# Last block of a recommendation kernel: its final scale on ScalarE and its store from ScalarE's queue, in place of VectorE and SP's queue

## The reference

```python
x_reg = input_data @ W_lin.T + b_lin
emb = input_data @ factors                      # 12500 -> 16
sum_squared = jnp.square(emb.sum(axis=1))
squared_sum = (jnp.square(input_data) @ jnp.square(factors)).sum(axis=1)
h = jax.nn.relu(emb @ W1.T + b1)                # 16 -> 128
h = jax.nn.relu(h @ W2.T + b2)                  # 128 -> 64
dnn_out = h @ W3.T + b3                         # 64 -> 1
x = x_reg + 0.5 * (sum_squared - squared_sum)[:, None] + dnn_out
x = 0.5 + jax.nn.sigmoid(x) * 5.0
return x.squeeze()
```

## Time and profile before

| what | value |
|---|---|
| three runs | 133.61, 133.75, 133.87 us |
| profiled execution, its own time | 133.76 us |
| its span, first to last instruction | 132.0 us |
| PE busy | 107.0 us (81%) |
| ACT busy | 61.5 us (47%) |
| DVE busy | 52.6 us (40%) |
| moved by DMA | 52.36 MB, mean 397 GB/s |
| mean granted TensorE clock | 0.974 |

### The profile page before, as it was taken

How to read it: one execution, slowest core, us unless ns; L and a number is a source line. 1 busy time by engine, 2 the same in 40 slices (tenths; PEclk the granted TensorE clock), 3 DMA queues, 4 the chain that set the end, 5 groups by cost and what they waited for, 6 DMA issues and landing times.

```text
span 132.0 us, 2607 instructions
## 1 busy us (share of the span) xinstructions
PE 107.0 (81%) x1123; PEld 34.6 (26%) x1123; DVE 52.6 (40%) x51; ACT 61.5 (47%) x52; POOL 15.7 (12%) x48
## 2 busy tenths in 40 slices
PE   6099969429979839749749979999998987989992
PEld 4012222002212112112112233322222112345881
DVE  0391063027036036046045016565351351576571
ACT  4030067029039039049048046868562561465851
POOL 3015000200010200200200110164530000000000
PEclk9999999995999999999977999999999999999999
DMA  3999899989999998998999999899999999999700
GB/s 106 413 531 417 377 477 472 407 387 467 427 387 462 457 427 387 457 437 387 467 457 427 387 457 447 377 432 412 452 407 407 462 415 417 418 404 411 302 26 1
DMA packets 3489, 52.36 MB, mean 397 GB/s; under 512 B 404, under 2 KB 536, under 8 KB 1560
## 3 DMA queue, kind: packets, MB, share of 16 engines
q1 hardware_dynamic: 3480, 52.23, 93.2%
HBM read 52.22 MB, written 0.00 MB: 396 GB/s over the span
## 4 chain that ended last, share of the span: by engine, by line
DMA 54%; PE 40%; SPq 2%; DVE 1%; issue 1%; ACT 1%
DMA xr<-in_x_pairs 43%; PE p_lin L506 34%; DMA xr<-in_x_end 11%; PE p_sq L506 2%; PE p_h L601 2%; SPq L273 1%; PE p_tot L506 1%; PE p_h L632 1%; PE p_tot L614 0%; DVE h L454 0%; DVE h L449 0%; SPq L267 0%; SPq L266 0%; PE p_tot L621 0%; SPq L265 0%
## 5 line engine op out<-in xcount | busy, mean ns | idle before, releaser
L327 ACT ACTIVATE sq<-xr 128x2560 f32<-128x2560 f32 x20 | 45.9, 2333 | 46.8 <-DMA xr<-in_x_pairs 38.8
L427 DVE TENSOR_TENSOR sq<-xr 128x1536 f32<-128x1536 f32 x20 | 34.6, 1761 | 53.7 <-DMA xr<-in_x_pairs 42.9
L506 PE MATMUL p_lin<-xr,wr 128*17 128x512 f32 x320 | 39.9, 638 | 15.6 <-DMA xr<-in_x_pairs 14.4
L506 PE MATMUL p_lin<-sq,wz 128*18 128x512 f32 x320 | 37.7, 592 | 0.0
L506 PEld LDWEIGHTS p_lin<-xr,wr 128*17 128x17 f32 x320 | 9.2, 102 | 44.5 <-issue 38.4
L307 POOL COPY wr<-hd 128x136 f32 (+1 forms) x20 | 9.3, 464 | 75.0 <-PE p_lin L506 75.0
L506 PEld LDWEIGHTS p_lin<-sq,wz 128*18 128x18 f32 x320 | 10.1, 98 | 25.8 <-issue 25.0
L506 PE MATMUL p_lin<-xr,hd 128*17 128x352 f32 (+1 forms) x128 | 10.0, 380 | 1.3 <-DMA xr<-in_x_end 1.3
L437 DVE TENSOR_TENSOR sq<-xr 128x1408 f32<-128x1408 f32 (+3 forms) x6 | 6.6, 1135 | 6.1 <-DMA xr<-in_x_end 6.1
L337 ACT ACTIVATE sq<-xr 128x1408 f32<-128x1408 f32 (+3 forms) x6 | 5.7, 983 | 6.3 <-DMA xr<-in_x_end 6.3
L506 PE MATMUL p_lin<-sq,ws 128*18 128x352 f32 x64 | 6.6, 459 | 0.0
(11 more groups left out here) (52 smaller groups left out, 40.8 us busy)
## 6 DMA issues: line engine op xcount, KB each, us to landing
xr<-in_x_pairs SPq DMA_DIRECT2D x8, 4096.0 KB, 21.9
xr<-in_x_groups SPq DMA_DIRECT2D x4, 2048.0 KB, 18.3
xr<-in_x_end SPq DMA_DIRECT2D x1, 2112.0 KB, 10.5
xr<-in_x_end SPq DMA_DIRECT2D x3, 640.0 KB, 12.0
xr<-in_x_end SPq DMA_DIRECT2D x1, 1760.0 KB, 14.3
xr<-in_x_end SPq DMA_DIRECT2D x1, 1056.0 KB, 12.4
hd<-in_head SPq DMA_DIRECT2D x1, 952.0 KB, 4.8
xr<-in_x_end SPq DMA_DIRECT2D x1, 704.0 KB, 13.7
```

The source lines that it names most:

```text
L327: nc.scalar.activation(sq[:, ring(s), BY_DVE:CHUNKS, :], xr[:, s, BY_DVE:CHUNKS, :], ACT.Square).then_inc(act_squared, 1)
L427: nc.vector.tensor_tensor(sq[:, ring(s), 0:BY_DVE, :], xr[:, s, 0:BY_DVE, :], xr[:, s, 0:BY_DVE, :], ALU.mult).then_inc(dve_squared, 1)
L506: return nc.tensor.matmul(out, lhsT, rhs, start=False, stop=False, skip_group_check=True)
```

## The change

For blocks 0 and 1 nothing is changed. For block 2, the last, VectorE's scale is taken out. ScalarE waits for its own sigmoid, computes Copy(5.0 * sg + 0.5) into `y`, waits for that, and issues the store itself, from its own DMA queue. SP's loop of stores is one shorter; its last wait still counts the landings of all three.

```diff
@@ sync
-            for k in range(len(BLOCKS)):
+            for k in range(LAST):
                 sp.wait_ge(y_ready[k], 1)
                 sp.dma_start(out[cols(k)].rearrange("(q b) -> q b", q=4), y[0:P:32, line(k)]).then_inc(y_stored, 16)
             sp.wait_ge(y_stored, 16 * len(BLOCKS))
@@ scalar
             nc.scalar.copy(qs[:, :], p_sq[:, 0:BLOCKS[LAST][1]]).then_inc(qs_ready, 1)
             sigmoid(2)
+            act.wait_ge(sg_ready[2], 1)
+            nc.scalar.activation(y[:, line(2)], sg[:, line(2)], ACT.Copy, bias=0.5, scale=5.0).then_inc(y_ready[2], 1)
+            act.wait_ge(y_ready[2], 1)
+            nc.scalar.dma_start(out[cols(2)].rearrange("(q b) -> q b", q=4), y[0:P:32, line(2)]).then_inc(y_stored, 16)
@@ vector
             layer1(2, p_h1[1], BLOCKS[2][1])
             layer2(2)
-            scale(2)
```

## The result

The changed kernel took 133.99 us (median of 20 runs, 133.85 to 134.23) against 133.75 us before (20 runs, 133.61 to 134.01). The ratio is 1.0017, with a 95% interval of 1.001 to 1.0024: slower by 0.24 us, within the 0.2% that I called no change, and clear of zero. The forecast was 133.91.

The account below looks back on a forecast made before the run. Input DMA (54%) and TensorE (40%) bound the kernel; only its serial 2.5 us tail could change. Scale +0.03, hand-overs 0, issue +0.13, landing 0 gave +0.16 us: 133.91, 8 in 10 from 133.55 to 134.40.

Parts of the forecast that it names:

- The place: Tail of 2.5 us behind TensorE's last adds at 129.47: all steps in series, each nanosecond counting in the kernel's time.
- The scale: Block 2's scale on ScalarE instead of VectorE: 215 ns for 185, +0.03 us, ends +0.02 and +0.11.
- The wait of an engine for itself: ScalarE's semaphore wait between its sigmoid and scale: 0.03 us as across engines, so 0; ends 0.03 less, 0.05 more.
- The hand-over to the DMA: From the scale's end to the store's issue: 0.04 us, taken the same on ScalarE, so 0.
- The queue: Last store on ScalarE's own queue: no gain, 0, since SP had nothing before it but its wait.
- The issue: ScalarE's issue of the last store, priced like SP's first store: 0.63 for 0.50, +0.13 us, ends -0.17 and +0.68.
- landing: From the last store's issue to its landing: taken as 0, low end -0.25 us (0.86 in place of 1.11).
- rival A: ScalarE's first DMA is dear: up to +0.71 us, named 134.18, deciding from an issue of 0.74 us; chance 0.41.
- The sum: All terms of the tail together: +0.16 us, 133.91 us, +0.12%, within the 0.27 us called the same.
- The closing barrier: Kernel's end: ScalarE's drain at about 130.6 instead of 129.5, 1.0 us before SP passes its wait, so not moved.

Follow-up runs that it names:

- one step more: Changed kernel plus one more ACTIVATE on ScalarE, copying y onto itself with a wait, between scale and store: 134.26 us, ratio 1.0031 to the kernel before.
- the two halves: Against the kernel before: ScalarE scales block 2, SP stores it, 133.88 us (1.0003); VectorE scales, ScalarE stores it, 133.92 us (1.0007).
- the second group: Changed kernel unaltered, run again beside the kernel before on the same chip: 133.99 us against 133.84, ratio 1.0006.

## Why the prediction was right, and where not

*The place.* Only the tail moved, and it is serial: confirmed, with one step more of 265 ns by forecast and 263 to 268 got out in the branch (2533 against 2270 and 2265).

*The scale, forecast +0.03.* It was 236 - 185 = 51 ns. My straight line through squares of 160 and 320 columns gave 215, and the Trainium skill's estimate (page "ScalarE: Activation LUTs", section "What ACT_TABLE_LOAD costs") 219; the measurement is above both, inside the range of 0.02 to 0.11.

*The wait of an engine for itself, forecast 0.* The scale starts 326 ns after the sigmoid's start on either engine: exactly 0. The hand-over to the DMA is 29 ns in both, and 25 and 32 in the two halves. Three engines in the tail cost nothing over one.

*The queue, forecast no gain.* SP's queue was free, and half the change with SP's store was the cheaper half. The page "DMA: Bandwidth & Descriptors" of the Trainium skill, section "Issuing engines are not separate DMA queues", promised at most a saved issue time; here even that was negative.

*The issue, forecast +0.13, landing 0.* The sum of the two was 127 ns, so the number was right. The reasoning was not, and the agreement is luck. I took the longer issue as the data's delay, by SP's first store with its 0.13 us. The issue took 1.10 us, 0.61 longer, far past the 0.74 that I named as rival A's point of decision and as its proof, and rival A's price didn't come. In the data a first store costs 84 to 90 ns, not the 0.13 of SP's issue, and ScalarE's queue 37 more for which I had no term; the two happen to add up to it. An issue's length and the start of its data are two quantities: the first grew by 608 ns, the second by 127. SP shows the same: 625 against 497 in the issue, 84 ns in the data.

*The sum, forecast +0.16.* By the trace 51 + 127 = 178 ns, and 183 in the branch. The medians say 0.24, with an interval of 0.13 to 0.32 from the ratio's, which holds both; in the second group they say 0.15. The span's part outside, 1.8 us, did not change.

*The closing barrier.* I had ScalarE's drain at 130.6, it came at 131.2; 0.6 us of slack in place of 1.0 before SP's branch, still no cost.

## What to carry to other kernels

A program's last few steps are serial, so price them by their records from one fixed event, not by medians. For a small store at the end, use a queue that has already done a store of the same form at a time when nobody waited, and don't move it to another queue if its own is idle. Where a store has to stand in the middle of an engine's list, put it behind long instructions of that engine and not ahead of them. Read from a DMA's issue when it begins and from the windows when its bytes move; the issue's length is no measure of the delay.

## What the runs showed of the hardware

ScalarE's first DMA of four partitions took 1.09 to 1.11 us to issue at any time, from 0.7 to 130 us, in either direction, and later ones 0.54 to 0.59; its first of 128 partitions took 0.40 to 0.41. SP's stores took 0.62 to 0.63 the first time, at 113, 128 or 130 us, and 0.50 to 0.51 later. ScalarE's used queue was still 37 ns slower to the data than SP's used one (1176 against 1139). The start of `y` came 31 to 33 ns after the sigmoid's end, on the same engine or the other. An issue on ScalarE that stands behind squares runs beside them; ahead of one it held it up for its 1.11 us and 0.40 of waiting around it.
